# First layer of a two-layer graph network: the gathered rows are added on VectorE, the target count moves to ScalarE, SiLU runs in place

## What is computed

```python
src, dst = (edge_index[0], edge_index[1])
msg_input = jnp.concatenate([h[src], h[dst], edge_feat], axis=-1)
messages = jax.nn.silu(msg_input @ W1 + b1) @ W2 + b2
agg = jax.ops.segment_sum(messages, dst, num_segments=h.shape[0])
upd_in = jnp.concatenate([h, agg], axis=-1)
h_new = jax.nn.silu(upd_in @ W3 + b3) @ W4 + b4
return h_new + h
```

## Time and profile before

| | us |
|---|---|
| median of 3 runs | 1888.09 (1885.48 to 1891.9) |
| span of the profiled execution | 1500.6 |
| POOL from its first gather to its last of the first layer | 22.49 to 1034.69 |
| second layer after the first | about 1039 to 1500.6 |

### The profile page before, as it was taken

One profiled execution on the slowest core, in us unless ns is written; L12 is line 12 of the kernel. 1 busy time (PEld: TensorE's weight loads), 2 busy tenths in 40 slices (PEclk: granted clock), 3 DMA queues, 4 the chain that ended last, 5 costly groups with the idle time before them and its releaser, 6 DMA issues.

```text
span 1500.6 us, 31339 instructions
## 1 busy us (share of the span) xinstructions
PE 1285.9 (86%) x8165; PEld 1063.6 (71%) x8165; DVE 1014.5 (68%) x2310; ACT 642.1 (43%) x1257; POOL 1107.0 (74%) x1164
## 2 busy tenths in 40 slices
PE   6788789778777889888888888885999999999992
PEld 6666667556556667767767776764899999998982
DVE  4678888677665565665566656643666888878866
ACT  2744556555555555555556555551111111111111
POOL 5777777777777777777777777777777777777771
PEclk9898889999998999999999999997999999999996
DMA  6533333333336454454455445433887778778731
GB/s 206 135 85 92 93 95 94 95 96 91 95 90 119 118 138 125 126 136 131 125 131 133 125 128 135 113 80 105 258 261 230 208 230 241 222 230 241 213 92 47
DMA packets 189124, 214.15 MB, mean 143 GB/s; under 512 B 60426, under 2 KB 149517, under 8 KB 189011
## 3 DMA queue, kind: packets, MB, share of 16 engines
q1 hardware_dynamic: 138399, 131.62, 28.9%
q0 software_dynamic: 36352, 74.52, 21.3%
q10 hardware_dynamic: 14260, 6.68, 1.6%
HBM read 202.74 MB, written 9.85 MB: 142 GB/s over the span
## 4 chain that ended last, share of the span: by engine, by line
POOL 42%; PE 32%; issue 15%; DVE 4%; DMA 4%; SPq 1%; ACT 1%; DVEq 0%; ACTq 0%; POOLq 0%
POOL gath L873 42%; PE bank L1434 9%; PE bank L1410 8%; PE bank L1362 4%; DMA gath<-src_term,src_col 2%; PE bank L1240 2%; PE bank L1250 2%; PE bank L1233 2%; PE bank L1421 1%; DMA T<-in_x 1%; DMA gath<-layer_input,src_col 1%; PE bank L1396 1%; PE bank L1383 1%; PE bank L1441 0%; PE bank L1456 0%
## 5 line engine op out<-in xcount | busy, mean ns | idle before, releaser
L873 POOL DMA_INDIRECT gath<-src_term,src_col x768 | 737.2, 960 | 234.2 <-issue 230.2
L873 POOL DMA_INDIRECT gath<-layer_input,src_col x336 | 329.6, 981 | 105.6 <-issue 100.6
L1240 PE MATMUL bank<-gath,ident 128*128 128x512 f32 x384 | 218.3, 652 | 114.5 <-DMA gath<-src_term,src_col 113.8
L1233 PEld LDWEIGHTS bank<-terms_r,terms_l 128*128 128x128 f32 x1568 | 209.4, 201 | 83.1 <-issue 69.2
L1233 PE MATMUL bank<-terms_r,terms_l 128*128 128x128 f32 x1568 | 219.6, 286 | 30.4 <-ACT msg L1022 22.0
L1923 DVE TENSOR_SCALAR_CACHE_REDUCE terms_l<-dst_bc,node_col 64x512 f32<-64x512 int32 x196 | 221.0, 1128 | 13.1 <-issue 7.2
L1250 PEld LDWEIGHTS bank<-oh,msg 128*128 128x128 f32 x1568 | 198.7, 202 | 26.9 <-issue 26.1
L1934 DVE TENSOR_TENSOR S<-S,bank 128x128 f32 x98 | 28.1, 286 | 270.2 <-PE bank L1252 178.2
L1250 PE MATMUL bank<-oh,msg 128*128 128x128 f32 x1568 | 202.3, 285 | 0.0
L1434 PE MATMUL bank<-S 128*128 128x288 f32 x672 | 170.0, 406 | 0.1
L1649 DVE TENSOR_TENSOR oh<-bank,dst_rel 128x1024 f32<-128x1024 f32 x140 | 169.8, 1213 | 0.0
(11 more groups left out here) (219 smaller groups left out, 1754.7 us busy)
## 6 DMA issues: line engine op xcount, KB each, us to landing
dst_bc<-in_dst SPq DMA_DIRECT2D x195, 128.0 KB
xT<-sorted_src SPq DMA_DIRECT2D x42, 512.0 KB
xs<-layer_input SPq DMA_DIRECT2D x136, 128.0 KB
gath<-src_term,src_col POOLq DMA_INDIRECT x768
terms_l<-layer_input SPq DMA_DIRECT2D x88, 128.0 KB
terms_r<-layer_input SPq DMA_DIRECT2D x88, 128.0 KB
msg<-layer_input SPq DMA_DIRECT2D x80, 128.0 KB
ef_s<-in_edge_attr SPq DMA_DIRECT2D x97, 64.0 KB
```

Source lines behind the costliest of these rows:

```text
L873: g.indirect_dma_start(out=to[:, j * D:(j + 1) * D], out_offset=None, in_=table[0:rows, :], in_offset=bass.IndirectOffsetOnAxis(ap=indices ...
L1233: mm(bank[h][:, j * D:(j + 1) * D], terms_l[:, u, h, j, :], terms_r[:, u, h, j, :], start=j == 0, stop=False)
L1240: mm(bank[h][:, :], ident[:, :], gath[:, slot, :], start=False, stop=True).then_inc(pre_ps, 1)
```

## The change

- `pre_sums` ends with the last product of `terms_l` and `terms_r`; the product of the identity with the gathered slot is gone (not for the two pairs from `x`), and so is its wait for the gather.
- A new stage of DVE, `add_rows`, lag 2, behind `one_hots`, waits for `sums_ps(k - 2)`, for the products, and for the gather, and writes `bank[h] + gath[slot]` to `msg`. For the two pairs from `x` it copies the bank.
- `messages` runs SiLU on `msg` in place, after `rows_added`.
- `windows` compares without `accum_out`. A new stage of ACT, `degrees`, lag 2, ahead of `messages`, copies those 64 partitions of `terms_l` with `accum_out` into `deg_col`, and to a scratch tile `pre`.
- POOL's wait before it fills a slot goes by `rows_added` in place of `pre_ps`; the bank of a group is free by `rows_added` in place of `msg_made`.
- Six semaphores of the preparation become three.

```diff
                     if g >= RING:
-                        pool.wait_ge(pre_ps, done(g - RING))
+                        pool.wait_ge(rows_added, done(g - RING))
...
+            def degrees(k, m, q):
+                act.wait_ge(sums_ps, done(k - DEEP))
+                for h in range(2):
+                    r = slice((1 - h) * W, (2 - h) * W)
+                    act.wait_ge(ohT_made, done(2 * k + h))
+                    act.wait_ge(deg_made, done(2 * k + h - 2))
+                    a.activation(pre[r, :].rearrange("p (j e) -> p j e", j=CH), terms_l[r, m % 2, h, :, :], ACT.Copy,
+                                 accum_out=deg_col[r, m:m + 1]).then_inc(deg_made, 1)
...
-                    act.wait_ge(pre_ps, done(g))
-                    act.wait_ge(sums_ps, done(k - 2))
-                    a.activation(msg[:, 2 * (m % 2) + h, :], bank[h][:, :],
-                                 ACT.Silu).then_inc(msg_made, 1)
+                    act.wait_ge(rows_added, done(2 * k + h))
+                    of = msg[:, 2 * (m % 2) + h, :]
+                    a.activation(of, of, ACT.Silu).then_inc(msg_made, 1)
...
-                  of_pair(1, edge_features), of_pair(0, window_x),
+                  of_pair(1, edge_features), of_pair(0, window_x), of_pair(2, degrees),
...
-                    pe.wait_ge(msg_made, done(g - 2))
+                    from_rows = isinstance(k, int) and k < FROM_X
+                    pe.wait_ge(rows_added, done(g - 2))
                     for j in range(CH):
-                        mm(bank[h][:, j * D:(j + 1) * D], terms_l[:, u, h, j, :], terms_r[:, u, h, j, :],
-                           start=j == 0, stop=False)
-                    if isinstance(k, int) and k < FROM_X:
+                        last = mm(bank[h][:, j * D:(j + 1) * D], terms_l[:, u, h, j, :], terms_r[:, u, h, j, :],
+                                  start=j == 0, stop=j == CH - 1 and not from_rows)
+                    if from_rows:
                         add_from_x(g, bank[h])
-                        continue
-                    slot = 2 * m + h
-                    pe.wait_ge(gathered[slot], 16 * CH * (q + 1))
-                    mm(bank[h][:, :], ident[:, :], gath[:, slot, :], start=False, stop=True).then_inc(pre_ps, 1)
+                    else:
+                        last.then_inc(pre_ps, 1)
...
+                pe.wait_ge(deg_made, done(2 * k + 1))
                 mm(bank[2 + u][0:1, PW:2 * PW], deg_col[:, m:m + 1], ident[:, :],
                    start=True, stop=True).then_inc(sums_ps, 1)
...
                 dve.wait_ge(pre_ps, done(2 * k - 3))
-                dve.wait_ge(sums_ps, done(k - DEEP))
+                dve.wait_ge(deg_made, done(2 * k - 3))
                 for h in range(2):
                     r = slice((1 - h) * W, (2 - h) * W)
                     ve_.tensor_scalar(terms_l[r, u, h, :, :],
                                       dst_bc[r, u, :].rearrange("n (p j) -> n j p", j=CH), node_col[r, ds(k, 1)],
-                                      None, ALU.is_equal, ALU.add, accum_out=deg_col[r, m:m + 1]).then_inc(ohT_made, 1)
+                                      None, ALU.is_equal).then_inc(ohT_made, 1)
+
+            def add_rows(k, m, q):
+
+                u = m % 2
+                dve.wait_ge(sums_ps, done(k - 2))
+                for h in range(2):
+                    slot = 2 * m + h
+                    to = msg[:, 2 * u + h, :]
+                    dve.wait_ge(pre_ps, done(2 * k + h))
+                    if isinstance(k, int) and k < FROM_X:
+                        ve_.tensor_copy(to, bank[h][:, :]).then_inc(rows_added, 1)
+                        continue
+                    dve.wait_ge(gathered[slot], 16 * CH * (q + 1))
+                    ve_.tensor_tensor(to, bank[h][:, :], gath[:, slot, :], ALU.add).then_inc(rows_added, 1)
...
-                  of_unit(9, ordered_norm0), of_pair(3, add_sums), (0, NPAIR, sort_edges),
+                  of_pair(2, add_rows), of_unit(9, ordered_norm0), of_pair(3, add_sums), (0, NPAIR, sort_edges),
```

More of the change, by code:

```diff
@@ L280, in build @@
         wef_ready = sem("wef_ready")
-        src_prep = sem("src_prep")
-        src_turned = sem("src_turned")
-        src_ready = sem("src_ready")
-        dst_prep = sem("dst_prep")
-        dst_turned = sem("dst_turned")
-        dst_ready = sem("dst_ready")
+        rows_prep = sem("rows_prep")
+        rows_turned = sem("rows_turned")
+        cols_ready = sem("cols_ready")
+        OF_SRC, OF_DST = 1, 2
         lo_made = sem("lo_made")
@@ L333, in build @@
         sums_ps = counter("sums_ps", "pe")
+        rows_added = counter("rows_added", "dve")
+        deg_made = counter("deg_made", "act")
         deg_added = counter("deg_added", "dve")
@@ L1132, in _, with turn_rows @@
             mm = nc.tensor.matmul
-            def turn_rows(rows_f, prep, banks_read, turned):
-                pe.wait_ge(prep, 1)
-                if banks_read:
-                    pe.wait_ge(banks_read, 1)
+            def turn_rows(rows_f, of):
+                pe.wait_ge(rows_prep, of)
+                if of > OF_SRC:
+                    pe.wait_ge(cols_ready, of - 1)
                 for q, n in ((0, P), (1, GT)):
@@ L1143, in turn_rows @@
                             rows_f[0:n, q, :].rearrange("g (p j) -> g j p", j=CH)[:, j, :], ident[0:n, 0:n])
-                last.then_inc(turned, 1)
+                last.then_inc(rows_turned, 1)
             pe.wait_ge(consts, 1)
@@ L1176, in _ @@
             blocks((0, turn_x), (1, terms), (0, only_at({
-                6: lambda: turn_rows(src_rows_f, src_prep, None, src_turned), 10: spread_bases})))
-            turn_rows(dst_rows_f, dst_prep, src_ready, dst_turned)
+                6: lambda: turn_rows(src_rows_f, OF_SRC), 10: spread_bases})))
+            turn_rows(dst_rows_f, OF_DST)
             pe.wait_ge(A_made, done(NB))
-            pe.wait_ge(dst_ready, 1)
+            pe.wait_ge(cols_ready, OF_DST)
             pe.wait_ge(base_ready, 1)
@@ L1526, in _, with cols_of @@
             ve_ = nc.vector
-            def cols_of(turned, column, last_p):
-                dve.wait_ge(turned, 1)
+            def cols_of(of, column, last_p):
+                dve.wait_ge(rows_turned, of)
                 for q, g0, n in ((0, 0, P), (1, P, GT - 1)):
@@ L1536, in cols_of, with to_float @@
                 return ve_.tensor_copy(column[0:last_p, (NG - 1) * CH:NG * CH], ps[0:last_p, n, :])
-            def to_float(rows, rows_f, landed, made):
+            def to_float(rows, rows_f, landed):
                 dve.wait_ge(landed, 16 * 4)
                 ve_.tensor_copy(rows_f[:, 0, :], rows[:, 0, :])
-                ve_.tensor_copy(rows_f[0:GT, 1, :], rows[0:GT, 1, :]).then_inc(made, 1)
+                ve_.tensor_copy(rows_f[0:GT, 1, :], rows[0:GT, 1, :]).then_inc(rows_prep, 1)
             def keep_A(b, u, t, nt):
@@ L1557, in least_dst @@
             def least_dst():
-                dve.wait_ge(dst_prep, 1)
+                dve.wait_ge(rows_prep, OF_DST)
                 ve_.tensor_reduce(lo[:, 0:1], dst_rows_f[:, 0, :], AX_X, ALU.min)
@@ L1622, in _ @@
             blocks((1, keep_A), (1, order_xT), (0, only_at({
-                4: lambda: to_float(src_rows, src_rows_f, src_in, src_prep),
-                6: lambda: cols_of(src_turned, src_col, P).then_inc(src_ready, 1),
-                7: lambda: to_float(dst_rows, dst_rows_f, dst_in, dst_prep), 8: least_dst, 9: diagonals,
+                4: lambda: to_float(src_rows, src_rows_f, src_in),
+                6: lambda: cols_of(OF_SRC, src_col, P).then_inc(cols_ready, 1),
+                7: lambda: to_float(dst_rows, dst_rows_f, dst_in), 8: least_dst, 9: diagonals,
                 11: window_bases})))
-            cols_of(dst_turned, dst_col, LAST_P).then_inc(dst_ready, 1)
+            cols_of(OF_DST, dst_col, LAST_P).then_inc(cols_ready, 1)
             relative_dst()
-            dve.wait_ge(src_ready, 1)
+            dve.wait_ge(cols_ready, OF_SRC)
             ve_.tensor_copy(iota_ps, iota_w[:, 0:PW]).then_inc(iota_kept, 1)
```

7 lines of the change are left out of this document (3 added, 4 removed).

## The result

The changed kernel took 2046.12 us (median of 4 runs, 2032.94 to 2057.42), the kernel before 1889.99 us (1885.48 to 1905.59, 4 runs): 1.0816 times, 95% interval 1.0753 to 1.0878. I had predicted 1908 and a range up to 1932. Faster, same and slower were given 0.04, 0.24 and 0.72; the direction is right and the size is eight times too small: 156 us in place of 20.

What follows compares the result with a forecast made beforehand. POOL's issuing of 800 gathers, 1.265 us each, was taken to bound the first layer. Only 20 us of stretched gathers counted, other terms 0: span 1500.6 to 1520.6, with 387.5 us kept on top 1888 + 20 = 1908 us; range 1886 to 1932.

Steps and rivals of the forecast that it cites:

- The runs' median lies 387.5 us above the profiled span, and I leave that as it is: Whole kernel: the 387.5 us between profiled span and timed runs was assumed to lie outside the instructions and stay unchanged.
- everybody else waits for it: First layer: it takes as long as POOL needs to issue its gathers, 10.12 us a pair; other engines wait.
- Cost on the path: 0: DVE in the first layer: its added work and its new wait for the gather were to cost nothing.
- the ring's 32 us of slack: Gather slots, needed again eight groups later: DVE may be about 32 us late before POOL stops.
- The lock: First layer: plain DVE compares under way hold back POOL's gathers, 196 × 0.10 = 20 us.
- The rival of the full lock: Every compare under way at a gather's start holds it until it ends: 40 us, or 49 in bad phase; chance 0.12.
- less than a whole instruction's worth: DVE compares against POOL gathers: the trace was read as showing a smaller delay than the skill's whole-instruction rule, half its sum.
- ScalarE's read of the sum: ACT's new counting copies: reading the accumulated sum was put at 0.08 us, as on DVE.
- The tail: End of the first layer: statistics ready some 3 to 4 us earlier, but POOL takes them no earlier; gain 0.
- VectorE's sums idled: DVE's new sums in the profile after: most of their idle time was to be put down to the gather.
- under 70%: PE in the first layer of the profile after: it was to be busy less than 70% of the time.
- The clock: PE's granted clock in the first layer: a little lower with PE busy less, at no cost.

Runs made afterwards that it cites:

- b_again: The kernel before, unchanged, on a quick machine: 1500.53 us.
- b_third: The kernel before, unchanged, profiled on a slow machine: 1936.0 us.
- add_only: The changed kernel, but the compare keeps its count and ScalarE counts nothing: 1503.03 us on a quick machine, 1.0016 times the kernel before.
- wait_only: The kernel before, with only a VectorE wait for the pair's finished products at the place of `add_rows`: 1934.60 us on a slow machine, ratio 1.0021.
- count_only: The kernel before, with the compare's count moved to ScalarE and the identity product kept: ratio 1.0126 on a quick machine, 0.9958 repeated on a slow one.
- both_counts: The changed kernel, with the compare's count given back into an unread column: 1506.75 us on a quick machine, 1.0014 times the kernel before.
- compare_twice: The changed kernel, with each plain compare made twice: 1527.64 us on a quick machine, 1.0151 times the kernel before.
- a_again: The changed kernel, unchanged, on a quick machine: 1518.99 us, 1.0124 times the kernel before.

## Why the prediction was wrong, and where it was right

**The step that failed** is the one in its sum, "The runs' median lies 387.5 us above the profiled span, and I leave that as it is". I took 1888 − 1500.6 for something outside the instructions and kept arguing from a span in which POOL bounds the first layer. But span and time belong together within 2 us wherever both are known of one execution: 1499.0 and 1500.9 in b_again, 1933.0 and 1934.9 in b_third, 2043.3 and 2045.3 in the changed kernel. The timed runs were made on a slow machine, and on such a one (b_third) POOL waits 291.5 us for slots in the first layer. There "everybody else waits for it" is false, and with it every cost that I had set to zero because POOL's issuing covers it. A difference of a fifth of the time between trace and runs should have been the first rival of all.

**The term that failed with it** is the cost of DVE's and PE's waits, "Cost on the path: 0". On the quick machines it holds: add_only 1.0016, at most 4 us. On the slow machines it is 7.4%, some 140 us, by the trace 1420.8 − 1283.7 = 137 us of the first layer. I had looked at who stands behind DVE's wait for the gather and at the ring's 32 us of slack. I had not looked at who stands behind the sum on the other side. The bank of a group was freed by ScalarE's SiLU before and is now freed by DVE, with the rest of DVE's work in the same order, and the SiLU itself now comes one hand-over later. The ring lets POOL run ahead; it gives PE, DVE and ACT nothing, since the same two banks serve every pair. That the loss comes by these edges is argued from the code, from the waits for the sum and from wait_only; how it divides among them is not shown.

**The lock** was right in kind and, with some luck, in size. Predicted: 196 × 0.10 = 20 us, the gathers' mean at 0.984 us, 800 gathers over about 1032 us. Measured on the quick machines: +18.5 and +22.9 us, 0.980 and 0.986, and 1027.7 us (1050.08 − 22.42). count_only and both_counts show that it is the count's absence. What I had wrong is the form of the price. I had interpolated 0.10 us a compare between compares of two other lengths; 18.5 / 196 = 0.094 and 22.9 / 196 = 0.117 are means over phases, and compare_twice shows that they are no price per compare. That they came so near is where the luck was. The rival of the full lock, 40 us, had the wait right and the price wrong: a held gather does wait until the compare ends, but it can be held at two moments only, where the rival let every moment count. The Trainium skill (SBUF — State Buffer, section "Who interferes with whom") has it that the engine that comes second fully blocks for the other's whole instruction. The runs agree with its list of forms, for the `tensor_scalar` that also writes out its accumulator does not contend and the plain one does; and they agree that the block lasts to the instruction's end (the 84 held gathers of a_again, each within 0.02 us), so that my reading of "less than a whole instruction's worth" out of averages was wrong. In the case for which the time was given, the lock cost nothing: it is covered there (count_only_2, 0.9958).

**ScalarE's read of the sum** was set at 0.08 us, as on DVE, and takes 0.185; that cost nothing that shows.

**The tail** came as predicted where POOL is the bound. In a_again, DVE and then POOL:

```profile
1046.20 0.25 DVE L2046 BATCH_NORM_AGGREGATE mv<-st 128x2 f32<-128x6 f32 x2
```

```profile
1049.13 0.95 POOL L873 DMA_INDIRECT gath<-layer_input,bridge_rows  x1 [0.30 <-issue]
1050.11 0.26 POOL L918 TENSOR_SCALAR var_eps<-mv 128x2 f32<-128x2 f32 x1
```

The statistics are ready at 1046.45, 3.6 us before POOL's last gather ends, where it was 2.45 us before the change, and POOL takes them no earlier. Two smaller marks of the same trace: VectorE's sums idled 94.7 us, 92.8 of it for the gather, as predicted; and PE was 72% busy in the layer (742.61 of 1027.66 us), where I had said under 70%.

**The clock** fell as expected and cost nothing that shows on the quick machines: 0.85 over the first layer in a_again against 0.94 before. On the slow machines it was 0.74 in the changed kernel and 0.85 in b_third, with PE busy less; PE's products take 0.325 us at the mean in the one and 0.314 in a_again, 0.327 in b_third and 0.286 in b_again. That is far too little for the difference between the machines, so the clock is not what makes them slow.

**Left open.** Why some machines are slow: PE's matmuls 0.70 us apart and the late answers to PE are what the traces show; whether both have one cause, what it is, and whether the recording of the trace has a part in it, they don't show. Of the sum's 7.4% there, its place in DVE's order is about half, and DVE's stop alone is none of it. How the rest divides among PE's wait for the bank, the SiLU's later start and PE's pauses within its products is not separated; for that, the kernel before would have to free its banks by DVE's wait with the identity product kept. No version was faster than the kernel before on both kinds of machine; count_only gave 0.9958 on a slow machine and 1.0126 on a quick one.

## What to carry to other kernels

Before anything is read from a trace, its span must agree with the time of the runs that are to be predicted; where it doesn't, the bound that it shows may not be theirs, and every "hidden behind" is worth nothing. When a sum moves to another engine, look at everything that waits for it, and not only at what it waits for: count the hand-overs that a piece of data passes, and ask what the kernel costs when each takes some microseconds. And a cheaper instruction can be dearer: the compare lost 0.44 us by dropping its count and took 20 us from another engine by it.

## What the runs showed of the hardware

- A plain compare on VectorE (0.69 us) holds a GpSimd gather until the compare ends, if it ends 0.14 to 0.60 us or 0.87 to 1.23 us after the gather's start; the gather is then longer by that time less 0.12 or 0.83 us: 84 gathers of a_again, 101 of count_only and 156 of compare_twice, all but one within 0.02 us. 38 gathers of a_again in which a compare ended 0.62 to 0.83 us after the start lost nothing. The same compare with a count, 1.13 us long, holds none (177 to 184 gathers started in one).
- The same program took 1500 to 1504 us on two machines and 1890 to 1942 us on others. There PE starts single products 0.70, 1.40 or 2.10 us apart (217 of 6725 distances; 2 on a quick machine). VectorE, idle and waiting for PE, goes on 5.5 us after PE's product in b_third and 0.20 us after it in b_again; PE, waiting for VectorE, goes on within 0.15 us on both kinds at the median.
- ScalarE's read of an activation's sum takes 0.185 us, VectorE's 0.079.
